# A fused state-space and feed-forward layer: residual and a low half on GpSimd, later rounding, four tiles moved ahead

## What is computed

```python
x = x + mamba(layernorm(x))
x = x + ffn(layernorm(x))

# mamba: 256 -> 2*512, causal depthwise conv of 4 taps, silu, then per state n of 16
h = exp(A[n] * dt) * h + dt * B[n] * xc        # a scan over time, 512 channels
y = sum_n h * C[n] + D * xc
return silu(y + res) @ W_out.T                 # 512 -> 256

# ffn, all weights -1, 0 or 1, with a scale per output column
h = silu(lin(x, w1)) * lin(x, w2)              # 256 -> 1024
h = gelu(lin(h, h1)); h = gelu(lin(h, h2))     # 1024 -> 1024, twice
return lin(h, w3)                              # 1024 -> 256
```

## Time and profile before

| | |
|---|---|
| median of 3 runs | 2812.95 us (2811.05 to 2813.61) |
| the profiled execution | 2812.52 us |
| its span, first to last instruction | 2810.7 us |
| granted TensorE clock, mean | 0.974 of full |
| PE busy | 2619.4 us, 93% |
| DVE busy | 2284.3 us, 81% |
| ACT busy | 1947.2 us, 69% |
| GpSimd busy | 1696.1 us, 60% |
| HBM | 70 GB/s over the span |

### The profile page before, as it was taken

How to read it: one execution, slowest core, us unless ns; L and a number is a source line. 1 busy time by engine, 2 the same in 40 slices (tenths; PEclk the granted TensorE clock), 3 DMA queues, 4 the chain that set the end, 5 groups by cost and what they waited for, 6 DMA issues and landing times. The chain is left out here.

```text
span 2810.7 us, 48687 instructions
## 1 busy us (share of the span) xinstructions
PE 2619.4 (93%) x17154; PEld 2338.5 (83%) x17154; DVE 2284.3 (81%) x2923; ACT 1947.2 (69%) x4070; POOL 1696.1 (60%) x1483
## 2 busy tenths in 40 slices
PE   6679999999999999999999999999977999999998
PEld 4558888888888888888888888888867888888887
DVE  4999999999999999999999999999983455555554
ACT  7888888888888888888888888888864322222221
POOL 3778888888888878888888888878862000000000
PEclk8889999999999999999999999999988999999999
DMA  6111212112111211212112112211131322222210
GB/s 228 43 43 54 68 58 76 58 57 65 58 57 62 69 61 59 68 58 76 58 58 64 58 57 64 67 61 61 62 116 64 116 77 90 84 82 90 90 61 31
DMA packets 130150, 198.74 MB, mean 71 GB/s; under 512 B 16368, under 2 KB 93296, under 8 KB 129904
## 3 DMA queue, kind: packets, MB, share of 16 engines
q1 hardware_dynamic: 129904, 195.57, 21.7%
HBM read 144.68 MB, written 50.86 MB: 70 GB/s over the span
## 5 line engine op out<-in xcount | busy, mean ns | idle before, releaser
L1137 DVE TENSOR_TENSOR_SCAN h<-banks,ub 128x512 f32<-128x512 f32 x1024 | 1200.9, 1206 | 39.2 <-ACT banks L1008 23.7
L758 POOL TENSOR_TENSOR ub<-u,b_row 128x1020 f32<-128x1020 f32 x512 | 1215.1, 2373 | 0.3 <-issue 0.2
L1150 DVE SCALAR_TENSOR_TENSOR acc<-banks,c_tok,acc 128x512 f32<-128x512 f32 x1024 | 723.0, 736 | 95.3 <-PE banks L1434 76.4
L1434 PE MATMUL banks<-ident,h 128*128 128x128 f32 x4096 | 613.5, 280 | 149.8 <-DVE acc L1150 75.1
L1008 ACT ACTIVATE banks<-dt,neg_a 128x510 f32<-128x510 f32 x1024 | 692.1, 683 | 59.5 <-DVE h L1137 55.5
L1434 PEld LDWEIGHTS banks<-ident,h 128*128 128x128 f32 x4096 | 489.5, 144 | 240.4 <-DVE h L1137 165.8
L1422 PE MATMUL banks<-act_high,h_rounded 128*128 128x256 f32 x2048 | 516.7, 292 | 11.8 <-POOL act_low L774 11.8
L1422 PE MATMUL banks<-act_low,h_rounded 128*128 128x256 f32 x2048 | 495.6, 281 | 0.0
L1422 PEld LDWEIGHTS banks<-act_high,h_rounded 128*128 128x128 f32 x2048 | 389.6, 190 | 14.2 <-issue 12.5
L1460 PE MATMUL banks<-act_low,h_rounded 128*128 128x512 f32 x1024 | 398.8, 389 | 0.0
L1460 PE MATMUL banks<-act_high,h_rounded 128*128 128x512 f32 x1024 | 398.6, 389 | 0.0
(11 more groups left out here) (116 smaller groups left out, 3983.5 us busy)
## 6 DMA issues: line engine op xcount, KB each, us to landing
b_row<-b_scratch SPq DMA_DIRECT2D x128, 512.0 KB, 4.1
z_scratch<-z_out SPq DMA_DIRECT2D x128, 256.0 KB, 2.1
zl<-z_scratch SPq DMA_DIRECT2D x32, 1024.0 KB, 8.0
x_sb<-in_x SPq DMA_DIRECT2D x32, 256.0 KB, 5.1
x_res<-in_x SPq DMA_DIRECT2D x32, 256.0 KB, 4.9
h_full<-in_h SPq DMA_DIRECT2D x2, 4096.0 KB, 17.8
x_scratch<-x_sb SPq DMA_DIRECT2D x32, 256.0 KB, 4.7
xr<-x_scratch SPq DMA_DIRECT2D x16, 512.0 KB, 4.8
```

The lines of the kernel that those rows point to most:

```text
L758: nc.gpsimd.tensor_tensor(ub[:, n % 2, :, 1:], u[:, :, 1:], b_row[:, n // QUARTER % 2, n % QUARTER:n % QUARTER + 1, 1:].to_broadcast([P, E ...
L1137: nc.vector.tensor_tensor_scan(h[:, n % 2, 2 * i:2 * i + 2].rearrange("p e t -> p (e t)"), banks[:, k % DECAYS, :], ub[:, n % 2, 2 * i:2 * ...
L1150: nc.vector.scalar_tensor_tensor(out=acc[:, par, q], in0=turned[q], scalar=c_tok[:, par, q, n:n + 1], in1=acc[:, par, q], op0=ALU.mult, op ...
L1434: last = nc.tensor.transpose(turned[q][:, e * P:(e + 1) * P], h[:, n % 2, e, q * P:(q + 1) * P], ident[:])
```

## The change

- The identity products with x_res go. ACT only copies the output bank into x1_sb (step 22); GpSimd adds x_res behind ub of state 11; ACT's `sums2` (step 24) makes the row sums from x1_sb, instead of together with the copy.
- `xT_low` moves from DVE to GpSimd. GpSimd can't read the bank, so ACT copies it a second time, into the new tile xT.
- Many places in the order lists move by one or a few steps.
- The late weights are rounded two pieces a state from state 9 on, instead of one a state from 5 on.
- Block 0's eight gelus and splits stand together in step 20 of the first body of `ending` (on DVE at step 30), with two table loads, and four of its eight h2 tiles stand in PE's list inside `ending`: tile 0 at the end of the first body, tile 1 before the h1 layer of the second, tiles 2 and 3 before that of the third.

```diff
+        xT = sb("xT", [P, KD, T], where=a_only)
...
         PE_AT = dict(
-            norm={28: ('xn',), 29: ('xp0.a', 'xp0.b'), 30: ('xp1.a',), 31: ('xp1.b',)},
-            front={0: ('conv0.a',), 2: ('conv0.b', 'conv0.c'), 3: ('conv0.d', 'conv1.a'), 5: ('conv1.b', 'conv1.c', 'conv1.d'), 11: ('ssm.a', 'ssm.b'), 13: ('dtc',), 23: ('acc0.a', 'acc0.b', 'acc0.c'), 25: ('acc1.a', 'acc1.b'), 26: ('acc1.c',)},
-            post={12: ('gT0',), 13: ('gT1',), 14: ('out.a',), 15: ('out.b',), 17: ('out.c', 'out.d')},
...
-        DVE_AT = dict(low2=56, gated=(87, 88, 89, 93))
-        ACT_AT = dict(sums=5, x1=23, sums2=24, logs=5, logs2=24, xn=31, xp=(0, 1), silu=(10, 26), ssm=16, z=17, soft=21, acc=(28, 30), gT=17, high2=35, high=(61, 64, 66, 67), z_out=(78, 80, 84, 89), a_dt=31)
-        POOL_AT = dict(normalize=4, normalize2=13, dt=13, u=15, low=(33, 36, 34, 35))
-        SP_AT = dict(x=0, x1=14, res=15, write_b=4, b=(14, 14, 1, 6), z_out=(35, 36, 42, 43))
+            norm={29: ('xn', 'xp0.a'), 31: ('xp0.b', 'xp1.a', 'xp1.b')},
+            front={0: ('conv0.a',), 1: ('conv0.b',), 2: ('conv0.c', 'conv0.d'), 3: ('conv1.a', 'conv1.b'), 4: ('conv1.c',), 5: ('conv1.d',), 10: ('ssm.a',), 11: ('ssm.b',), 13: ('dtc',), 23: ('acc0.a', 'acc0.b', 'acc0.c'), 25: ('acc1.a', 'acc1.b', 'acc1.c')},
+            post={10: ('gT0',), 13: ('gT1',), 14: ('out.a',), 16: ('out.b',), 17: ('out.c', 'out.d')},
...
+        DVE_AT = dict(gated=(88, 88, 90, 93))
+        ACT_AT = dict(sums=4, x1=22, sums2=24, logs=6, logs2=28, xn=31, xp=(2, 5), silu=(10, 26), ssm=16, z=18, soft=21, acc=(27, 31), gT=17, high2=40, high=(66, 66, 67, 70), z_out=(77, 80, 85, 89), a_dt=31)
+        POOL_AT = dict(low2=21, x1=11, normalize=9, normalize2=17, dt=14, u=15, low=(33, 36, 34, 35))
+        SP_AT = dict(x=0, x1=12, res=12, write_b=4, b=(11, 14, 1, 6), z_out=(35, 40, 41, 44))
...
-        FIRST_ROWS = [(CHUNKS + 2, 2 * o) for o in range(KH)]
+        FIRST_ROWS = [(CHUNKS, 20) for o in range(KH)]
+        IN_TAIL = {(CHUNKS, 30): (0,), (CHUNKS + 1, 6): (1,), (CHUNKS + 2, 6): (2, 3)}
...
+            def post(c, n):
+                if n == POOL_AT["x1"]:
+                    wait_taken(pool, "out", c)
+                    pool.wait_ge(xres_in, 16 * (c + 1))
+                    rows = x1_sb[:, c % 2].rearrange("p q d -> p (q d)")
+                    nc.gpsimd.tensor_tensor(rows, rows, x_res[:].rearrange("p q d -> p (q d)"), ALU.add).then_inc(x1_ready, 1)
...
+                if s == POOL_AT["low2"]:
+                    pool.wait_ge(xT_high_ready, c + 1)
+                    wait_taken(pool, "yn", c)
+                    nc.gpsimd.tensor_tensor(xT_low[:], xT[:], xT_high[:].bitcast(F32), ALU.subtract).then_inc(xT_low_ready, 1)
...
             def sums2(c):
-                wait_taken(act, "out", c)
-                act.sem_inc(x1_ready, 1)
+                act.wait_ge(x1_ready, c + 1)
...
+                for q in range(NT):
+                    last = nc.scalar.activation(xn2[:, q], x1_sb[:, c % 2, q], ACT.Copy, accum_out=row_sum2[:, q:q + 1])
+                last.then_inc(sum2_ready, 1)
+                act.wait_ge(sum2_ready, c + 1)
...
                 if n == ACT_AT["x1"]:
-                    add_rows(c)
+                    after(act, x1_out[c % 2], 16 * (c // 2))
+                    after(act, xn2_ready, c - 1)
+                    take("out", c, x1_sb[:, c % 2].rearrange("p q d -> p (q d)"), bank("out", c))
...
                     nc.scalar.activation(xT_high[:].rearrange("p k t -> p (k t)"), bank("yn", c), ACT.Copy).then_inc(xT_high_ready, 1)
+                    take("yn", c, xT[:].rearrange("p k t -> p (k t)"), bank("yn", c))
...
-                    if c == CHUNKS - 1 and 5 <= n < 5 + len(late_pieces):
+                    if c == CHUNKS - 1 and 9 <= n < 9 + LATE // 2:
                         act.wait_ge(late_in, 32)
-                        nc.scalar.activation(*late_pieces[n - 5], ACT.Copy).then_inc(rounded_late, 1)
+                        for piece in late_pieces[2 * (n - 9):2 * (n - 8)]:
+                            nc.scalar.activation(*piece, ACT.Copy).then_inc(rounded_late, 1)
...
                 if (c, n) in FIRST_ROWS:
-                    first(0, FIRST_ROWS.index((c, n)))
+                    nc.scalar.preload_act_table_set("gelu_and_others")
+                    for o in range(KH):
+                        first(0, o)
+                    nc.scalar.preload_act_table_set("natural_log_exp_and_others")
...
-                            pe.wait_ge(xres_in, 16 * (c + 1))
-                        if quarter % 2 == 0:
-                            nc.tensor.matmul(into[:, q * DIM:(q + 1) * DIM], ident[:], x_res[:, q], start=True, stop=False)
-                        for e in (range(0, 1), range(1, ET))[quarter % 2]:
+                        for e in range(ET // 2 * (quarter % 2), ET // 2 * (quarter % 2 + 1)):
...
+            def in_tail(c, n):
+                for o in IN_TAIL.get((c, n), ()):
+                    if o == 0:
+                        pe.wait_ge(rounded_late, 10)
+                        for q in range(NT):
+                            pe.wait_ge(y_added[q], NS * CHUNKS)
+                    second_layer(0, o)
...
-                        second_layer(blk, o)
+                        if blk >= 1 or o >= IN_TAIL_JOBS:
+                            second_layer(blk, o)
```

More of the change, by code:

```diff
@@ L812, in exp_rows @@
                 nc.scalar.activation(rstd[:], log_var[:], ACT.Exp, scale=-0.5).then_inc(rstd_ready, 1)
-            def add_rows(c):
-                wait_full(act, "out", c)
-                after(act, x1_out[c % 2], 16 * (c // 2))
-                after(act, xn2_ready, c - 1)
-                for q in range(NT):
-                    last = nc.scalar.activation(x1_sb[:, c % 2, q], bank("out", c)[:, q * DIM:(q + 1) * DIM], ACT.Copy, accum_out=row_sum2[:, q:q + 1])
-                last.then_inc(freed("out", c), 1)
             def sums2(c):
-                wait_taken(act, "out", c)
-                act.sem_inc(x1_ready, 1)
+                act.wait_ge(x1_ready, c + 1)
                 after(act, xn2_ready, c)
```

61 lines of the change are left out of this document (29 added, 32 removed).

## The result

The changed kernel takes 2766.4 us (median of 4 runs, 2765.27 to 2768.03) against 2812.5 in the same comparison: ratio 0.984, 95% interval 0.982 to 0.985. The profiled run has a span of 2764.8 us, 45.9 less than the 2810.7 of before.

The account below looks back on a forecast made before the run. The prediction took PE, with ACT as a second bound behind it, to bound the chunks. Terms -5 (points 1 to 3), -14 (clock), -8 (rounding) and +2 (tiles) sum to -25: 2812.5 to 2787 us, range 2768 to 2806.

Parts of the forecast that it names:

- Points 1 to 3: Scan chunks: residual off PE, ACT's ledger and low half off DVE together give 0.2 us a chunk, -5 us.
- The stretch gives nothing instead of 1.2: ACT's states 8 to 13: stays 23.8 us, so PE's list, 1.2 us a chunk shorter, pays nothing there.
- ACT's ledger of its own operations: ACT's states 8 to 13: 1.51 us out and 1.53 in, leaving 23.8 us.
- PE was the bound: Rival for the chunks: residual off PE pays 1.2 x 31 us instead of 5, total 2755; 12%.
- Point 6: Chunks' first transposes: PE's 2.22 us pause shrinks to 0.5, ten lower-clock pieces go, -14 us, bounds 0 and -17.
- Point 4: Chunks: GpSimd's two added operations, about 1.28 us each, fit its free 11.2 us, cost 0; upper bound 1.28 a chunk.
- Point 7: Last chunk: later rounding removes the late-weights wait, leaves about 6 us for ACT's decay; -8 us, bounds -5 and -11.
- Point 8: Tail and second part: four early tiles fill holes, but PE pauses 13 us before block 1; +2 us, bounds -4, +5.
- Slower rival: Chunks: ACT's sum waits at step 24 for GpSimd's late residual add, 1.28 us a chunk; +34, 2846 us; 8%.
- wrong if ACT waits for the residual: Chunks: sign against the forecast, ACT waiting for GpSimd's residual add; no size given.
- The rule of the Trainium skill that the prediction cited: PE: waits between bursts of matmuls put the array back to the lower clock each time.

Follow-up runs that it names:

- norm_no_identity: Kernel before the change, with the first projection at its new places and PE's identity products left out (residual missing, timing only): 2778.1 us.
- norm_residual_logs: Kernel before, with the first projection's new places, the residual on GpSimd, and log and exp of the variance behind ACT's second silu visit: 2796.9 us.
- low_on_dve_early: Changed kernel with the low half back on DVE near its old place, without ACT's second copy or GpSimd's subtraction: 2773.3 us, 63.64 a chunk.
- pe_product: Changed kernel with PE's two identity products a chunk back at their old place, each overwritten by what follows: 2788.0 us.
- out_places: Changed kernel with four of PE's pieces of states 5 to 8 back at their earlier steps: 2764.9 us, 63.50 a chunk.
- norm_alone: Kernel before, with only the places of the first projection and its evacuation changed: 2794.2 us, period 64.26.
- low_alone: Kernel before, with only the low half of the normalized rows moved from DVE to GpSimd (behind state 2): 2835.3 us.
- residual_alone: Kernel before, with only the residual moved to GpSimd and ACT's sums to step 24, log and exp at their old place: 2815.8 us.
- round_early: Changed kernel with the late weights rounded one piece a state from state 5 of the last chunk again: 2772.1 us.
- no_tiles: Changed kernel with no tile of block 0 inside the tail, all eight behind the last h-layer: 2765.5 us.
- act_early: Changed kernel with an extra ACT copy of 512 columns in state 2: period 63.51 us a chunk, 3 us in the median outside the steady chunks.
- norm_places: Changed kernel with the first projection and its evacuation back at their old places and steps: 2877.5 us.
- no_identity: Kernel before, with PE's two identity products a chunk left out (residual missing, timing only): 2810.8 us.

## Why the prediction was wrong, by its steps

- **Points 1 to 3 (-5 forecast, -20 measured) is the step that failed.** The stretch was rightly placed at ACT, and the low half off DVE gives 0.13 us a chunk, as said. What failed is "The stretch gives nothing instead of 1.2": it gives 0.61 us of the 0.77 (27.33 to 26.72), and the rest of the chunk the other 0.16. ACT's ledger of its own operations was nearly right (one copy took 0.48 of ACT's time, start to next start, not the 0.60 of its row). But I booked ACT's waits for PE as a mere 0.48 and took the rest for an unbroken row. The two copies of gT advance ACT, from their start to the next start, by 1.30 us before and 0.95 after, a wait that no bracket lists. The wait ahead of z_out was larger than its bracket, too: the decay in front of it advances ACT by 1.25 us in the kernel before and by 0.61 in the changed one, 0.64 less. So PE held ACT up by about 1.0 us in the row that I had summed, and not by 0.48. The stretch also starts earlier than that row, at the first visit's table load, and holds a wait for PE's ssm product (0.50 before, 0.21 after). An engine whose chain contains waits for another isn't the bound alone: what shortens or reorders PE's list can shorten ACT's stretch. norm_no_identity shows 0.56 us a chunk for the products, two thirds of their 0.87.
- **"PE was the bound", the rival at 12%**, missed to the other side: its -37 us for these points is 17 too much, the forecast's -5 is 15 too little. That its total, 2755, lies nearer to 2766.4 is luck. PE's products pay because they lie inside ACT's stretch, as waits of ACT; in states 1 and 2 they pay 0.33 of 0.87.
- **Combination.** Of the three parts tried alone in the chunk only the projection's places give something: -19, +2 for the residual, +22 for the low half. Their sum has nothing to do with the -42 that the chunks gained together. The parts that the forecast reasoned about cancel: 64.26 to 64.40 with the residual and the logs, 0.13 back for the low half. The 0.76 us between norm_residual_logs and low_on_dve_early come with the other places, as waits of ACT for PE that go. They need the products' absence as well, for pe_product loses 0.83 of them again. Which place it is stays open: out_places excludes three, and the others (PE's conv pieces at the chunk's start, its pieces of w1, w2 and the h-layer, ACT's z step and its evacuations) were not tried one by one.
- **The first chunks**, for which the sum has no term, gave -7.1 us, 4.6 of them with the projection's places (norm_alone). Point 6 named two slow pieces there and left them to its bound; they are 2.7 of the 4.6. Up to the sixth b_u the mean granted clock is 0.91 before, 0.92 in norm_alone and 0.93 after; how the other 4.4 of the 7.1 us divide between the clock and the shorter chunk was not tested.
- **Point 4 (GpSimd free)** was right in size for the change, and for a reason that I hadn't given: place, not load. low_alone has only one of the two operations and loses 22 us.
- **Point 6 (-14)** was right in size: -14.7 in norm_alone, 34.6 - 26 x 0.77 = 14.6 in the changed kernel. The pause shrank to 1.1 us, not to 0.5. That the long pause alone makes the pieces isn't shown: residual_alone has the pause of 2.22 us and no piece.
- **Point 7 (-8)**: -6.3 between the traces, 5.7 by round_early. The wait for the weights went. A wait of about 6 us for ACT's decay ahead of state 13 was forecast; DVE's wait there is 5.20 us and ends with PE's transposes (the row at 2065.04). ACT is behind it all the same: the product ahead of the transposes in PE's list waited until 2061.22 for a bank of ACT's silu visit, and the decay itself starts only at 2065.49.
- **Point 8 (+2)**: +0.7 and +1.4 between the traces, +0.9 by no_tiles; the pause of 13 us and the slow restart (+2.3) are as forecast.
- **Slower rival** (ACT's sum waits for GpSimd's residual): the profile lists such a wait only once, 1.40 us in the tail. But in the ordinary chunks of all kernels with this addition ACT's sum starts 0.03 us after the addition ends (once 0.08, in act_early), wherever else work was put in; the addition itself starts 0.08 us after ACT's copy has ended. It is on the chain. In the changed kernel it costs little: the decay in front of the sum, at 778.18, advances ACT by 0.70 us instead of 0.61. So the forecast's sign "wrong if ACT waits for the residual" did come, at about 0.1 us a chunk.

```profile
777.54 1.30 POOL L772 TENSOR_TENSOR x_sb<-x_sb,x_res 128x512 f32<-128x512 f32 x1 [0.69 <-ACT x_sb L804]
```

```profile
778.88 0.42 ACT L835 ACTIVATE xn<-x_sb 128x256 f32<-128x256 f32 x1
```

## What to carry to other kernels

In a software pipeline with orders written by hand, find the stretch whose length moves one to one with the period (here ACT between two table loads; of the sixteen kernels in which it was read, the rest is 36.8 to 36.95 us in fourteen, and low_alone and norm_places differ) and cost each edit by what it does to that stretch, waits for others included. Take an operation's advance, start to next start, rather than its duration, and compare it with the same operation elsewhere: that is how hidden waits show. Work moved ahead of a stage whose own inputs arrive by a longer chain is worth nothing until that chain is shortened: ordering block 1's rows first gave 7 us, four tiles moved gave none without it. And compare the start of an operation with the end of what it reads: a wait of a tenth of a microsecond that comes in every chunk stands in no list of waits.

## What the runs showed of the hardware

- **The clock piece depends on more than the pause.** PE's pause at the chunk's first transposes is 2.22 us in the kernel before, in no_identity and in residual_alone. The first has a piece at the lower level in ten of 26 chunks, the second in 22, the third in none (its period is 64.84, and it has a second pause of 1.10 us). low_alone has the pause too, and pieces in 12; norm_places has it, and pieces in all 26. In the other fifteen kernels the pause is 1.1 us, and none has a piece in the 26 chunks. So in these chunks no piece came without the long pause, but a rule "a pause this long costs the clock" doesn't come out of this; what decides is open. The rule of the Trainium skill that the prediction cited (TensorE: Matmul & The Clock Gate, HAM oscillation) agrees with norm_places and block 1's restart and doesn't tell the first three apart.
- **Restart after a pause of PE in the second part**: three tiles take 13.23 us after 13.2 us of pause, 13.21 after 6.3, 12.65 after 3.3, and 10.9 without one. Halving the pause gave back the pause, not the restart. The granted clock accounts for it: in the changed kernel it is 0.50 over the first 4.43 us, and half of these is 2.2. In the other two it is 0.50 over 4.41 and 3.25 us.

```profile
2195.23:2199.66 4.43, 4.43 (x11) 3.46 (x12) 1.91 (x4) 0.00 (x0) 0.00 (x0) 0.50 0.00 0
```

- **GpSimd holds up DVE's splits, which read two operands from SBUF.** A split of 0.69 us took 1.74 when GpSimd's residual addition had started just ahead of it:

```profile
2103.12 1.29 POOL L772 TENSOR_TENSOR x_sb<-x_sb,x_res 128x512 f32<-128x512 f32 x1 [19.09 <-ACT x_sb L804]
```

```profile
2103.23 1.74 DVE L1213 TENSOR_TENSOR act_low<-zl,act_high 128x512 fp32r<-128x512 f32 x1
```

The split ends 0.56 us after the addition does, so it ran almost wholly behind it. It isn't a single case: every kernel based on the changed one has one such split of 1.72 to 1.75 us in the tail. The kernel before has two, of 1.65 and 1.64 us (2193.65 and 2196.74), beside GpSimd's low halves; there the cast between them, with one operand, took 1.49 us instead of 0.42. The Trainium skill (GPSIMD Engine Reference, Specifications) names DVE instructions with two SBUF inputs among those that contend with GpSimd for the shared SBUF interfaces; these splits agree. In the chunks, where DVE's scans and additions read one operand from PSUM, GpSimd's two added operations left their durations as they were (scan 1.205 us, addition 0.735).
